# Constant matmuls into a free PSUM bank during TensorE's pauses in the routes, the combinations and at the attention's begin

## The reference

```python
    # --- layer 0 (adj_ffn) ---
    x = x + _L0_gnn_ref(_layernorm(x, axis=-1), adj, L0_gnn_W)
    x = x + _L0_ffn_ref((_layernorm(x, axis=-1))[None], L0_ffn_router_w, L0_ffn_router_b, L0_ffn_W1, L0_ffn_b1, L0_ffn_W2, L0_ffn_b2)[0]
    ...
    idx = jnp.argmax(logits, axis=-1)                      # layer 0: 1 of 32 experts, H = 64
    top2_vals, top2_idx = jax.lax.top_k(probs, 2)          # layer 1: 2 of 8 experts, H = 512
    topk_vals, topk_idx = jax.lax.top_k(gate_logits, TOP_K)  # layer 2: 2 of 8 experts, H = 512
    scores = jnp.where(adj[:, None, :] == 0, -jnp.inf, scores)   # layer 3: attention, 4 heads of 64
```

## Time and profile before

| | |
|---|---|
| median of 3 runs | 2124.05 us (2116.95 to 2125.85) |
| the profiled execution | 2119.9 us, its span 2118.1 us |
| TensorE busy | 1856.5 us (88%), 15581 matmuls |
| VectorE, ScalarE, GpSimd busy | 1511.2, 1129.3, 456.5 us |
| mean granted TensorE clock | 0.942 of the upper level |
| the chain that ended last | TensorE 65%, VectorE 19%, ScalarE 5%, issue 4%, DMA 3%, GpSimd 2% |

### The profile page before, as it was taken

How to read it: one execution, slowest core, us unless ns; L and a number is a source line. 1 busy time by engine, 2 the same in 40 slices (tenths; PEclk the granted TensorE clock), 3 DMA queues, 4 the chain that set the end, 5 groups by cost and what they waited for, 6 DMA issues and landing times.

```text
span 2118.1 us, 41965 instructions
## 1 busy us (share of the span) xinstructions
PE 1856.5 (88%) x15581; PEld 1259.1 (59%) x15581; DVE 1511.2 (71%) x3199; ACT 1129.3 (53%) x2228; POOL 456.5 (22%) x532
## 2 busy tenths in 40 slices
PE   6999486999999999966994899849967999999998
PEld 3788353788888888755772688737754222222344
DVE  6877655677767767775676677555666788899776
ACT  6566386633433435534784566436656445455476
POOL 0000575101010103304772011137620000002010
PEclk9999787999999999977997999969988999999999
DMA  7999455479898879965677566152232433322100
GB/s 211 342 345 352 142 173 183 174 249 343 307 331 287 324 265 373 402 237 183 206 244 262 147 181 204 62 197 91 89 115 75 124 96 114 91 79 80 57 18 36
DMA packets 236570, 412.55 MB, mean 195 GB/s; under 512 B 20303, under 2 KB 188879, under 8 KB 217616
## 3 DMA queue, kind: packets, MB, share of 16 engines
q1 hardware_dynamic: 213108, 361.52, 50.3%
q0 software_dynamic: 13760, 39.68, 6.1%
q10 hardware_dynamic: 9504, 8.65, 1.2%
HBM read 316.02 MB, written 93.78 MB: 193 GB/s over the span
## 4 chain that ended last, share of the span: by engine, by line
PE 65%; DVE 19%; ACT 5%; issue 4%; DMA 3%; POOL 2%; SPq 0%; ACTq 0%; DVEq 0%; POOLq 0%
PE ps L2972 9%; PE ps L1144 9%; PE ps L1146 9%; PE ps L1145 9%; PE ps L2978 5%; PE ps L296 4%; PE ps L298 4%; PE ps L297 4%; PE ps L2604 3%; PE ps L2606 2%; DVE BIG L3172 2%; DVE bst L533 1%; DVE BIG L1715 1%; DMA BIG<-expert_out 1%; PE ps L2577 1%
## 5 line engine op out<-in xcount | busy, mean ns | idle before, releaser
L1144 PE MATMUL ps<-R,BIG 128*128 128x256 f16 (+1 forms) x1764 | 482.3, 273 | 3.0 <-ACT BIG L1610 2.4
L1146 PE MATMUL ps<-R,BIG 128*128 128x256 f16 (+1 forms) x1764 | 479.8, 272 | 0.0
L1145 PE MATMUL ps<-R,BIG 128*128 128x256 f16 x1764 | 479.4, 272 | 0.0
L2972 PE MATMUL ps<-BIG 128*64 128x452 f32 x1056 | 230.8, 558 | 22.6 <-DVE BIG L3172 20.4
L3172 DVE SCALAR_TENSOR_TENSOR BIG<-BIG 128x904 f32<-128x904 f32 x176 | 198.9, 1192 | 34.4 <-PE ps L2978 23.8
L1144 PEld LDWEIGHTS ps<-R,BIG 128*128 128x128 f16 x1764 | 170.6, 97 | 29.5 <-issue 3.0
L1145 PEld LDWEIGHTS ps<-R,BIG 128*128 128x128 f16 x1764 | 172.5, 98 | 20.5
L1146 PEld LDWEIGHTS ps<-R,BIG 128*128 128x128 f16 x1764 | 170.7, 97 | 23.3
L2972 PEld LDWEIGHTS ps<-BIG 128*64 128x64 f32 x1056 | 64.3, 136 | 181.5 <-issue 137.1
L3052 ACT ACTIVATE BIG<-X,BIG 128x64 f32<-128x64 f32 x264 | 70.2, 337 | 170.2 <-PE ps L2978 170.2
L296 PE MATMUL ps<-X,BIG 128*128 128x256 f16 (+1 forms) x568 | 137.7, 255 | 3.9 <-ACT X L2631 3.7
(11 more groups left out here) (486 smaller groups left out, 4378.9 us busy)
## 6 DMA issues: line engine op xcount, KB each, us to landing
BIG<-adj_split SPq DMA_DIRECT2D x63, 1376.0 KB, 9.4
BIG<-in_adjT SPq DMA_DIRECT2D x29, 1408.0 KB, 9.9
BIG<-in_adj SPq DMA_DIRECT2D x22, 1408.0 KB, 10.6
BIG<-in_adjT SPq DMA_DIRECT2D x66, 452.0 KB, 3.3
adj_split<-BIG SPq DMA_DIRECT2D x21, 1376.0 KB
XX<-in_f SPq DMA_DIRECT2D x70, 256.0 KB, 7.6
experts_split<-XX SPq DMA_DIRECT2D x64, 256.0 KB
BIG<-experts_split SPq DMA_DIRECT2D x16, 1024.0 KB, 13.3
```

The source lines that it names most:

```text
L1144: pe.matmul(out[:, 0:n], pr[:, 0, k, :], h[:, k, 0:n], start=start, stop=False)
L1145: pe.matmul(out[:, 0:D], pr[:, 0, k, :], l[:, k, 0:D], start=False, stop=False)
L1146: return pe.matmul(out[:, 0:n], pr[:, 1, k, :], h[:, k, 0:n], start=False, stop=stop)
L2972: pe.matmul(ps[rs, 2 * (h // 2) + c, 0:CW], self.G[:, u, h * HF:(h + 1) * HF], self.PT[:, u, h, cs], start=start, stop=stop)
```

## The change

A helper `keep(pe, b, n)` issues n matmuls of `one2` by `sel2` (128 by 128 by 256 columns) into bank b of PSUM. It is called at 21 places with 893 matmuls in all. They are fixed numbers: none waits for anything beyond what TensorE waits for there, and nothing waits for them. New are a semaphore `pl` that VectorE sets in the route once the positions are shifted, and waits ahead of some calls (`ev`, `e1`, `xe`, `pl`) which make sure that the bank is free or place the call in time.

```diff
--- before.py
+++ after.py
@@ -298,6 +298,11 @@
             return pe.matmul(out, al, bh, start=False, stop=stop)
 
 
+        def keep(pe, b, n):
+
+            for _ in range(n):
+                pe.matmul(ps[:, b, 0:2 * P], one2[:, :], sel2[:, :], start=True, stop=True)
+
         LC = Stage("const", ld=0, v=0, p=0, id=0, x0=0, x1=0, x2=0, x3=0)
         small = [(cols[:, :], "cols"), (rowsf[:, :], "rows"), (b2f[:, :], "b2"), (sel2[:, :], "sel2"),
                  (lt[:, :], "lt"), (one2[:, :], "one2"), (ident16[:, :], "ident16"),
@@ -929,6 +934,8 @@
                         project(j // 2)
                     if 0 <= i - 7 < PR:
                         linear(i - 7)
+                    if i == 3:
+                        keep(pe, 0, 20)
                     if 0 <= i - 1 < PR:
                         turns(pe, s, i - 1, 2 + (i - 1) % 2)
                     if i >= 10:
@@ -1080,7 +1087,11 @@
                     j = i - 1
                     if 0 <= j < PR:
                         turn_in(j)
+                        if j == 0:
+                            keep(pe, 7, 25)
                         turns(pe, s, j, 2 + j % 2)
+                s.wait(pe, "xe", PR - 1)
+                keep(pe, 1, 95)
 
             def columns(self, dst, j):
                 return dst[:, :, 2 * j * P:2 * (j + 1) * P].rearrange("p f (a c) -> p a f c", a=2)
@@ -1276,6 +1287,7 @@
                 self.done = [self.st.end(n) for n in ("sr0", "sr1", "sr2", "w0", "w1", "w2", "w3", "lg")]
                 self.ready = [self.st.end(n) for n in ("w0", "w1", "w2", "w3", "lg")]
                 self.freed = [self.st.end(n) for n in ("used", "w0", "w1", "w2", "w3")]
+                self.read = self.st.end("ev")
 
             def pool(self, pool):
                 s = self.st
@@ -1330,6 +1342,10 @@
                         mm = three(pe, out, pr, k, HAh, HAl, D + 1, k == 0, k == KT - 1)
                     mm.then_inc(s["used"], 1)
                 for t in (KT - 2, KT - 1):
+                    if t == KT - 1:
+                        s.wait(pe, "ev", KT - 1)
+                        after(pe, LC)
+                        keep(pe, 0, 30)
                     rows.turn(pe, s, t, 0)
                     rows.logits(pe, s, t)
 
@@ -1439,6 +1455,7 @@
                 self.done = [self.st.end(n) for n in ("sr0", "sr1", "sr2", "lg", "w0", "w1", "w2", "w3")]
                 self.ready = [self.st.end(n) for n in ("w0", "w1", "w2", "w3", "lg")]
                 self.freed = [self.st.end(n) for n in ("used", "rl", "cb", "w0", "w1", "w2", "w3", "d4")]
+                self.read = self.st.end("e1")
                 self.counted = [self.st.end("cb")]
                 self.stored = Kept(self.st.end("d4"))
 
@@ -1967,7 +1985,7 @@
                 self.i, self.E, self.kind, self.prod = i, E, kind, prod
                 self.A = 1 if kind == "argmax" else 2
                 self.J, self.G = TILES[E], GROUPS[E]
-                self.st = Stage("route", lm=1, v=2 - self.A, a={"argmax": 0, "softmax": 2, "top2": 2}[kind], mk=3 - self.A, rk=4 - self.A, oh=self.A, ix=1,
+                self.st = Stage("route", lm=1, v=2 - self.A, a={"argmax": 0, "softmax": 2, "top2": 2}[kind], mk=3 - self.A, rk=4 - self.A, pl=1, oh=self.A, ix=1,
                                 cw=1, tb=2, sel=32 if i == 0 else 16 * 9)
                 self.done = [self.st.end("cw"), self.st.end("sel")]
                 self.indexed = [self.st.end("ix")]
@@ -1997,6 +2015,8 @@
 
             def pe(self, pe):
                 s, E = self.st, self.E
+                pe.wait_ge(*self.prod.read)
+                keep(pe, 1, (62, 48, 40)[self.i])
                 s.wait(pe, "mk", 1)
                 n, m = PR * E, self.mask16()
                 for t in range(KT):
@@ -2014,8 +2034,13 @@
                 if self.A == 1:
                     s.wait(pe, "mk", 2)
                     pe.matmul(ps[0:1, 5, 0:WORDS[E0]], number16[:, :], digits[:, :], start=True, stop=True).then_inc(s["rk"], 1)
+                    keep(pe, 1, 25)
                     s.wait(pe, "v", 1)
                     self.words = expert_words(pe, E0)
+                else:
+                    keep(pe, 1, 40)
+                s.wait(pe, "pl", 1)
+                keep(pe, 1, 20)
                 J = self.J
                 for a in range(self.A):
                     s.wait(pe, "oh", a + 1)
@@ -2193,7 +2218,7 @@
                 link(v.tensor_scalar(posf[:, 0:A, KT - 1], posf[:, 0:A, KT - 1], padbig[:, 0:1], None, ALU.add))
 
                 link(v.tensor_copy(posu[:, 0:A, :], posf[:, 0:A, :]))
-                v.tensor_scalar(posl[:, 0:A, :], posu[:, 0:A, :], 7, None, ALU.logical_shift_right)
+                v.tensor_scalar(posl[:, 0:A, :], posu[:, 0:A, :], 7, None, ALU.logical_shift_right).then_inc(s["pl"], 1)
                 link(v.tensor_scalar(posu[:, 0:A, :], posu[:, 0:A, :], P - 1, None, ALU.bitwise_and))
                 high, low = (hl16[:, i, 0:A * KT] for i in range(2))
                 v.tensor_copy(high, posl[:, 0:A, :].rearrange("p a t -> p (a t)"))
@@ -2404,6 +2429,7 @@
                     sel = selE[0:2 * E0, dyn(e[j], P)]
                     pe.matmul(ps[:, 4 + u, 0:D], sel, b2h[0:2 * E0, 0, :], start=False, stop=True).then_inc(s["ym"], 1)
 
+                keep(pe, 1, 28)
                 turn(0)
                 turn(1)
                 for z, n in self.route.done:
@@ -2417,6 +2443,7 @@
                     if j + 2 < J:
                         hidden(j + 2)
                     result(j)
+                keep(pe, (J - 1) % 2, 100)
 
             def act(self, act):
                 self.route.st.wait(act, "v", 1)
@@ -2606,7 +2633,9 @@
                             mm = pe.matmul(ps[:, 6 + j % 2, 0:D], hl2[:, u, t, rows], w[:, 0], start=False, stop=t == HT - 1)
                         mm.then_inc(s["ym"], 1)
 
+                keep(pe, 1, 40)
                 turn(0)
+                keep(pe, 1, 10)
                 turn(1)
                 for z, n in self.route.done:
                     pe.wait_ge(z, n)
@@ -2618,6 +2647,7 @@
                     if q + 1 < Q:
                         hidden(q + 1)
                     result(q)
+                keep(pe, (Q - 1) % 2, 120 if self.i == 1 else 60)
 
             def act(self, act):
                 after(act, self.route)
```

## The result

Timed in turns on the same chip, the change gives 2125.42 us (median of 20 runs, 2121.09 to 2129.4) and the kernel before 2122.18 us (20 runs, 2116.95 to 2125.85). The ratio is 1.0013, with a 95% interval of 1.0007 to 1.0019: slower by some 2.8 us (1.5 to 4.0), which is no change by the bound of 0.5% and near to the forecast of 2124.3 us. The profiled execution took 2126.44 us with a span of 2124.6 us. Single executions of one kernel spread over 8 us, so the 6.5 us between the two profiled spans are not the effect of the change, and I read from the two traces only distances between the same instructions of one place.

A forecast was written before the change was run, and what follows sets the result against it. TensorE, 65% of the chain that ended last, was taken as the bound, with its clock and late starts. Terms +2.5 - 0.6 - 1.0 + 0 - 0.7 = +0.2 us on 2119.9, plus 4.2 for the median: 2124.3, range 2114 to 2135.

The forecast's parts named there:

- 30 ahead of the last turn: Layer 0, before route 0: matmuls in a 4.2 us pause, partly at the lower clock; +0.3 us, bounds 0 and +2.2.
- 62 ahead of the ranking: Route 0: matmuls taking 6.8 or 13.2 us in a 9.5 us pause; taken as 0, bounds 0 and +3.7.
- Ranking: Route 0: the ranking's own matmuls run faster if the clock is still high; -0.4 us, at most 1.1 gained.
- 25 ahead of the register loads: Route 0: the sequencer runs ahead, so the loads need not wait for these matmuls; 0, bounds 0 and +4.1.
- rival 3: Route 0: the sequencer waits for the 25, so register loads start later; about +2.7 us, 2127.0 us, chance 0.20.
- 20 behind the loads: Route 0: no pause left, so they lengthen the path, less faster index matmuls; +3.0 us, bounds +1.2 and +4.3.
- 28 ahead of the first turn, 0; experts' begin, -0.4: Layer 0: matmuls fit a 4.5 us pause, 0; experts begin faster by the clock, -0.4 us of at most 2.7.
- Layer 1: Route 1 and its experts' begin: faster index and first experts' matmuls; full gain -3.6 us, taken as -0.6.
- Layer 2: Route 2 and its experts' begin: the same gains as in layer 1; full -2.7 us, taken as -1.0.
- The combinations: Calls behind the experts, in C1 and C2: vectors, gathers and memory rows bound these; 0, C0 at most -3.0 us.
- The attention: Attention's begin: 95 matmuls leave 3.4 us of a 13.8 us pause; -0.7 us, at most -1.6.
- Rival 1: Whole kernel: remaining pauses don't lower the clock, all full gains come; -13.5 us, 2110.6 us, chance 0.10.

The follow-up runs named there:

- held: Changed kernel with pauses filled more closely, such as 118 matmuls ahead of the attention, and route 0's 20 replaced by 4 beside each register load; 2121.85 us, ratio 1.0005.
- only_ends: Changed kernel keeping only the added matmuls behind the experts, in C1 and C2 and ahead of the attention (100, 120, 60, 20, 25, 95); 2123.81 us, ratio 1.0012.
- ends_again: The same kernel as only_ends, run once more; 2125.39 us, ratio 1.0019 to the kernel before.
- only_routes12: Changed kernel keeping only the added matmuls of routes 1 and 2 and of their experts' begins; 2122.26 us, ratio 0.9997.
- beside_loads: Changed kernel without the 20 matmuls behind route 0's register loads, with 4 behind each of the 13 loads instead; 2121.13 us, ratio 0.9996.

## Why the prediction was right, and where it was not

The time came out 1.1 us over the forecast and within its range, no change that matters, as the likeliest case had it. That it is so near is luck in part. The forecast put +0.2 us on a median of three runs, 2124.05, and twenty runs of the kernel before give 2122.18, 1.9 lower; the change itself was to cost 0.2 us and cost 2.8 (1.5 to 4.0). What was right is the loss, the 20 matmuls on the path of route 0. What failed is the other side of the sum: the 3.1 us (0.4 + 0.4 + 0.6 + 1.0 + 0.7) that the clock was to give back are shown nowhere.

By its terms, each measured as a distance in the profiled executions. Null, which has the waits but no added matmul, differs from the kernel before by some tenths itself, and a term counts only where the change differs from both.

- *30 ahead of the last turn, +0.3.* From the last L1231 to the route's first L2084 VectorE takes 235.33 to 237.59 = 2.26 us before, 2.44 in null and 235.12 to 237.68 = 2.56 with the change: +0.1 to +0.3. The 30 took 5.10 us, mostly at the lower clock. In held they cost 1.3 to 1.5.
- *62 ahead of the ranking, 0.* They ended 2.8 us before VectorE let the ranking go.
- *Ranking, -0.4.* From L2084 to the cast of `eid` 16.78 us became 16.26. But null has 236.49 to 252.72 = 16.23 without any added matmul, so this is not the clock's. Only held got under it.
- *25 ahead of the register loads, 0.* Right, by the loads at 254.1; rival 3 is refuted for 25 and true for 60.
- *20 behind the loads, +3.0.* +2.65 in one execution, +4.08 in another. The place, the missing pause and the size were read rightly from the 1.66 us of "issue". In the changed kernel the clock rose during the 20, so L2049 took 1.21 us.
- *28 ahead of the first turn, 0; experts' begin, -0.4.* The first turn still waited 1.3 us for its gather, and the turn that stands on the chain comes as long after the indices as before: 273.21 - 268.30 = 4.91 us, as 270.98 - 266.07 = 4.91. From the indices to the fourth add of C0 the trace has 96.4 in place of 96.9 us, but null has 95.9 without any added matmul, so none of it is the clock's.
- *Layer 1, -0.6.* From the indices to the second L2670 of the experts 984.51 - 964.97 = 19.54 became 988.38 - 969.58 = 18.80, which looks like the forecast. It is not shown to be the change's: the same distance is 18.57 in only_ends and 18.78 in ends_again, which add nothing in route 1 or at its experts' begin, and 20.46 in only_routes12, which has the calls there and where the second turn waited 4.43 us for its gather. In the changed kernel the first experts' matmul comes only 0.15 us earlier (977.24 - 964.97 = 12.27, 981.70 - 969.58 = 12.12), and the clock rises 4.0 us behind it (985.7) and not 5.3 (982.5). Nothing came from the index matmuls: the second L2049 had a remaining pause of 2.45 us and ran at the lower clock, 2.02 us as before, where the prediction looked for about 1 us in one of the two routes.
- *Layer 2, -1.0.* Mis-sized. The first L2670 comes 0.7 us earlier against the indices (14.86 became 14.14; 14.71 in null), but the third only 0.2 (18.78 became 18.61; 18.82 in null). What TensorE gained there was taken back within two steps by the engines behind it. And the 40 ahead of the ranking ended late here, against what the prediction had said of `mk`: the ranking began 0.4 us behind VectorE's last operation, before 0.1.
- *The combinations, 0.* Their turns still wait for rows; C0's low stretch is as before in kind, 361.0 to 371.3. But only_ends and ends_again are slower by 0.12 and 0.19%, some 2.5 to 4 us, and the prediction had put these calls at nothing. Beside_loads and held have the same calls and come at 0.9996 and 1.0005. So the term is in doubt, and no mechanism is found by which the calls would cost.
- *The attention, -0.7.* Nothing came: behind the remaining 3.44 us the first eight L3002 took 3.28 us, as before 3.27.

```profile
1623.82 10.53 PE L304 MATMUL ps<-sel,one 128*128 128x256 f16 x95
1637.80 3.28 PE L3002 MATMUL ps<-BIG 128*64 128x452 f32 x8 [3.44 <-DVE BIG L3202]
```

Against null, layer 0 gives 0.1 + 0.0 + 2.5 = +2.6 us, nearly all of it the 20 matmuls, and the ratio says +2.8. With the 0.8 and 0.2 us of layers 1 and 2, which are not shown to be the change's, it would be +1.7. The forecast's terms gave +0.2.

Rival 1, the clock that holds, was priced at -13.5 us. The change did not hold it, as the prediction expected. Where held did, it got -1.1 at the ranking (-0.6 against null) and -1.5 at the attention, about as priced, but -0.2 and -0.6 of 1.0 each at the index matmuls, and nothing at the experts; it paid 1.3 us or more for its 30 and 0.6 in route 2, and ended at 0.05% slower (0.04% faster to 0.14% slower). Half of TensorE's busy time in the low stretches was an upper bound that no kernel here came near. As 25 us of 2118 it is 1.2%, so it did not yet agree with a penalty under 1%, as the prediction said; what held got out of it does. Whether a way exists to begin the experts at the upper clock without matmuls in their path was not found. Rival 2 did not occur: the added matmuls raised the clock like others, and none but the 20 ended late by more than some 0.3 us. What was to show it, showed: the high part between two low ones, a clock up by 0.032 where I had said a hundredth or two, the index matmuls behind the 20. Their start against the first load moved from 8.6 us (254.6 to 263.18) to 12.2 (254.1 to 266.27), 3.6 later. The starts of the 20 are on average 0.17 us apart, not 0.21.

No version beats the kernel before by more than its interval: beside_loads, 0.9996, is the change without the cost of the 20.

## What to carry to other kernels

Before you fill a pause, ask what ends it. Where it is "issue", an engine's own sequencer is at work (here 13 register loads of some 0.65 us each), and whatever is put behind it is path; put it beside. A clock that is low where TensorE waits for others anyway costs little, and half of the busy time under it is a bound far from what comes back. A gain that is summed over begins of stages must be followed one tile further, to see whether the next engine keeps it. And read each gain in a kernel that lacks the cause as well: two of the gains that this change seemed to bring stand in kernels without its matmuls.

## What the runs showed of the hardware

- TensorE's sequencer reached register loads at once with 25 matmuls queued ahead of them, 14 of which had not started; with 60 it reached them 3.4 us late, when 18 had not started (one execution each).
- Pauses of one length may or may not cost the clock: 2.05 us at 2008 us left it high before and lowered it in held; 1.81 us left it high and 2.45 lowered it in route 1 of the changed kernel:

```profile
962.57 1.18 PE L2049 MATMUL ps<-X,XX 128*128 128x100 f16 x22 [1.81 <-DVE X L2238]
966.21 2.02 PE L2049 MATMUL ps<-X,XX 128*128 128x100 f16 x22 [2.45 <-DVE X L2238]
...
978.83 1.03 PE L2604 MATMUL ps<-ident,X 128*128 128x128 f16 x8 [2.07 <-DMA X<-rows_split,idxg]
```

- I had taken remaining pauses of two to three us as even odds. In the changed kernel those of 2.45, 2.07 and 3.44 us all have lower-clock work right behind them, and behind the 2.75 us ahead of the ranking (247.07) the clock fell at 248.4.
- A transfer that took 1.2 us longer stood ahead of a loss of 4.0 us, through a pause behind which the clock fell in dense work, in P1 of ends_again. At the same place the clock stayed high behind pauses of 1.24 to 1.88 us in four kernels and fell behind 1.92, 2.14 and 2.48 us in three others; elsewhere, as above, it stayed high behind 2.05.
